# Edge loop of a graph network: products of two tiles in one VectorE instruction each

## What is computed

```
tpw = mlp(edge_feats)                      # per edge, 4 x 128
w1, w2, w3, w4 = jnp.split(tpw, 4, axis=-1)
s0, s1 = x0[sender], x1[sender]            # 128 and 128 x 3
y0, y1 = edge_attrs[:, 0:1], edge_attrs[:, 1:4]
p1 = w1 * s0 * y0
p2 = (w2 * s0)[:, :, None] * y1[:, None, :]
p3 = w3[:, :, None] * s1 * y0[:, None, :]
p4 = w4 * jnp.einsum('eum,em->eu', s1, y1) / SQRT3
msg0 = jax.ops.segment_sum(concat(p1, p4), receiver)
msg1 = jax.ops.segment_sum(concat(p2, p3), receiver)
```

## Time and profile before

| | |
|---|---|
| median of three runs | 1691.36 us (1691.3 to 1697.8) |
| the profiled execution, span from first to last instruction | 1690.4 us |
| PE busy | 1478.5 us, 87% |
| DVE busy | 1306.6 us, 77% |
| ACT busy | 739.0 us, 44% |
| POOL busy | 498.2 us, 29% |
| mean granted TensorE clock | 0.946 |
| first and last L2072 of the edge loop | 698.9 and 1055.4 us |

### The profile page before, as it was taken

How to read it: one execution, slowest core, us unless ns; L and a number is a source line. 1 busy time by engine, 2 the same in 40 slices (tenths; PEclk the granted TensorE clock), 3 DMA queues, 4 the chain that set the end, 5 groups by cost and what they waited for, 6 DMA issues and landing times.

```text
span 1690.4 us, 24268 instructions
## 1 busy us (share of the span) xinstructions
PE 1478.5 (87%) x7869; PEld 805.5 (48%) x7869; DVE 1306.6 (77%) x2051; ACT 739.0 (44%) x1580; POOL 498.2 (29%) x496
## 2 busy tenths in 40 slices
PE   2888998367888787899999999979999999999997
PEld 1465445213333335566555565855544444444443
DVE  8786999997999997499898999697577656632232
ACT  1285666267555555355454555441244333402000
POOL 1788888710011012356555664000000000002000
PEclk9988999678999997799999999979999999999999
DMA  4101000143121102466565667000111201220000
GB/s 143 42 6 9 6 7 7 36 146 114 43 68 40 65 16 82 129 184 183 165 183 165 182 184 148 1 1 26 50 50 50 70 30 58 66 74 1 13 19 30
DMA packets 66890, 122.06 MB, mean 72 GB/s; under 512 B 12753, under 2 KB 31299, under 8 KB 66702
## 3 DMA queue, kind: packets, MB, share of 16 engines
q0 software_dynamic: 23408, 59.71, 14.1%
q1 hardware_dynamic: 41976, 57.57, 10.5%
q10 hardware_dynamic: 1446, 4.03, 0.7%
HBM read 105.85 MB, written 15.23 MB: 72 GB/s over the span
## 4 chain that ended last, share of the span: by engine, by line
PE 53%; DVE 16%; POOL 14%; issue 10%; ACT 4%; DMA 2%; DVEq 1%; ACTq 0%; POOLq 0%
PE PS L1240 18%; POOL recs L656 14%; PE PS L1116 8%; DVE arena L1923 6%; PE PS L1205 5%; PE PS L1306 5%; PE PS L1102 5%; DVE arena L1919 3%; ACT arena L1578 3%; PE PS L1291 2%; PE PS L1302 2%; PE PS L1167 1%; DVE cnt_d L1704 1%; DVE arena L2123 1%; PE PS L976 1%
## 5 line engine op out<-in xcount | busy, mean ns | idle before, releaser
L1240 PE MATMUL PS<-arena 128*125 128x512 f32 x640 | 275.0, 592 | 0.0
L656 POOL DMA_INDIRECT recs<-arena x170 | 244.3, 1437 | 89.9 <-issue 89.0
L1578 ACT ACTIVATE arena<-arena,gslot 128x32 f32<-128x32 f32 x832 | 185.1, 308 | 172.5 <-PE PS L1116 89.6
L1116 PE MATMUL PS<-arena 128*32 128x128 f32 (+1 forms) x3328 | 235.0, 311 | 16.2 <-issue 8.0
L721 POOL DMA_INDIRECT arena<-xup,gidx x208 | 197.5, 949 | 147.6 <-issue 69.9
L1116 PEld LDWEIGHTS PS<-arena 128*32 128x32 f32 x3328 | 176.9, 111 | 127.1 <-issue 68.6
L1028 PE MATMUL PS<-arena 125*128 125x512 f32 (+1 forms) x480 | 190.5, 534 | 44.1 <-DVE arena L1923 43.9
L2072 DVE TENSOR_TENSOR arena<-PS,arena 128x768 f32<-128x768 f32 x208 | 196.7, 946 | 0.0
L1240 PEld LDWEIGHTS PS<-arena 128*125 128x125 f32 x640 | 120.1, 188 | 154.6 <-issue 154.1
L1028 PEld LDWEIGHTS PS<-arena 125*128 125x128 f32 x480 | 86.0, 191 | 148.4 <-issue 78.0
L728 POOL CAST arena<-cnt_s 125x1250 f32<-125x1250 uint16 x10 | 12.5, 1302 | 473.1 <-PE PS L1240 473.1
(11 more groups left out here) (341 smaller groups left out, 2149.9 us busy)
## 6 DMA issues: line engine op xcount, KB each, us to landing
arena<-in_spline_wT SPq DMA_DIRECT2D x16, 1024.0 KB, 5.4
arena<-uv_rows SPq DMA_DIRECT2D x14, 610.4 KB
arena<-h_rows SPq DMA_DIRECT2D x26, 256.0 KB
h_rows<-arena SPq DMA_DIRECT2D x24, 256.0 KB, 2.8
arena<-xup,gidx POOLq DMA_INDIRECT x208
recs<-arena POOLq DMA_INDIRECT x170
xup<-arena SPq DMA_DIRECT2D x10, 250.0 KB
out<-x_sb SPq DMA_DIRECT2D x10, 250.0 KB
```

What stands on the lines that cost most here:

```text
L656: pool.indirect_dma_start(out=recs, out_offset=bass.IndirectOffsetOnAxis(pos[:, c:c + 1], 0), in_=rec[:, c, :], in_offset=None).then_inc(s ...
L1116: ins = t.matmul(PS[quad * DB:(quad + 1) * DB, bank, o0 * MUL:o0 * MUL + w], sel4[:, s, v * DB:(v + 1) * DB], prod[:, s, c0 * MUL:c1 * MUL ...
L1240: return t.matmul(PS[:NP, y2_bank(half, b), :], lhs[:, (k * HB + b) * NP:(k * HB + b + 1) * NP], w[:, k * D:(k + 1) * D], start=(first and ...
L1578: ins = A(sel4[:, s, y * DB:(y + 1) * DB], eq4[:, m // 4, s * DB:(s + 1) * DB], ACT.Copy, scale=gslot[:, par, c + R_Y + y:c + R_Y + y + 1])
```

## The change

`products(m)`, which made the products of one tile with two instructions of 256 and 768 elements, becomes `pair_products(k)`, which makes those of a pair with two instructions of 512 and 1536 elements. Their PSUM banks (0, 1 or 6, 7), their slots in `ring` and their halves of `prod` lie side by side, so one access pattern with one more dimension covers both tiles. It waits for both tiles' gathers and for both path weights, and counts `s_prod_ok` up by two at its end. The comparison stays on DVE, ahead of each second pair. `two_groups` now issues the products of pair k + 1, then the sums of both tiles of pair k. Nothing is changed in `add_sums`, nor in the loops of PE, ACT, POOL and SP. Besides, the counters s_xt1, s_xt2, s_xt3 and s_cols2 go away: those waits count on from s_xt and s_cols with an offset (x1_transposes, linear_up, x2_transposes, x3_transposes, evac_T, x2_in, x3_in, and L1617, L2128); and three helper functions that nothing called are deleted.

```
-            def products(m, par, n, n_pair, n_gath):
-
-                s = m % 4
-                if m == 0:
+            def pair_products(k, par, n, n_pair, n_gath):
+
+                m, s = 2 * k, 2 * k % 4
+                if k == 0:
                     dve.wait_ge(s_gidx_ok, n_pair)
-                if m % 4 == 0:
+                if k % 2 == 0:
                     dve.wait_ge(s_sel_ok, n + (2 * TP - 4))
...
-                xg = ring[:, m, :].rearrange("p (q n) -> p q n", q=4)
-                w = PS[:, (0, 1, 6, 7)[s], :].rearrange("p (q n) -> p q n", q=4)
-                pr = prod[:, s, :].rearrange("p (h q n) -> p h q n", h=2, q=4)
+                xg = ring[:, m:m + 2, :].rearrange("p t (q n) -> p t q n", q=4)
+                b0 = (0, 6)[k % 2]
+                w = PS[:, b0:b0 + 2, :].rearrange("p t (h g n) -> p t h g n", h=2, g=2)
+                pr = prod[:, s:s + 2, :].rearrange("p t (h q n) -> p t h q n", h=2, q=4)
                 dve.wait_ge(s_gath[m], n_gath)
-                dve.wait_ge(s_tpw_ps, n + (2 - m % 2))
-                v.tensor_tensor(pr[:, :, 0, :], w[:, 0:3:2, :], xg[:, 0:1, :].to_broadcast([128, 2, MUL]), ALU.mult)
-                v.tensor_tensor(pr[:, :, 1:4, :], w[:, 1:4:2, :].unsqueeze(2).to_broadcast([128, 2, 3, MUL]),
-                                xg[:, 1:4, :].unsqueeze(1).to_broadcast([128, 2, 3, MUL]), ALU.mult).then_inc(s_prod_ok, 1)
+                dve.wait_ge(s_gath[m + 1], n_gath)
+                dve.wait_ge(s_tpw_ps, n + 2)
+                v.tensor_tensor(pr[:, :, :, 0, :], w[:, :, :, 0, :], xg[:, :, 0:1, :].to_broadcast([128, 2, 2, MUL]), ALU.mult)
+                v.tensor_tensor(pr[:, :, :, 1:4, :], w[:, :, :, 1, :].unsqueeze(3).to_broadcast([128, 2, 2, 3, MUL]),
+                                xg[:, :, 1:4, :].unsqueeze(2).to_broadcast([128, 2, 2, 3, MUL]), ALU.mult).then_inc(s_prod_ok, 2)
...
             def two_groups(i, par, last=False):
-                for m in range(TP):
-                    if m + AHEAD < TP:
-                        products(m + AHEAD, par, i * (2 * TP) + (TP * par + m + AHEAD), None, i * 32 + 16 * (par + 1))
+                for k in range(GT):
+                    if k + 1 < GT:
+                        pair_products(k + 1, par, i * (2 * TP) + (TP * par + 2 * k + 2), None, i * 32 + 16 * (par + 1))
                     elif not last:
...
-                    if m % 4 == 0:
-                        word = dve.value_load(gpk[0:1, m // 4, bass.ds(i * 2 + par, 1)], min_val=0, max_val=64 ** 4 - 1)
-                    add_sums(m, i * (2 * TP) + (TP * par + m), word)
...
+                    if k % 2 == 0:
+                        word = dve.value_load(gpk[0:1, k // 2, bass.ds(i * 2 + par, 1)], min_val=0, max_val=64 ** 4 - 1)
+                    for m in (2 * k, 2 * k + 1):
+                        add_sums(m, i * (2 * TP) + (TP * par + m), word)
```

More of the change, by code:

```diff
@@ L733, in _ @@
             t = nc.tensor
[L735 to L755, removed]
             def uv_transposes(src, nr, done, b0):
@@ L1048, in x1_transposes @@
                 if b >= 2:
-                    pe.wait_ge(s_xt1_cp, b - 1)
+                    pe.wait_ge(s_xt_cp, NB + b - 1)
                 for k in range(4):
@@ L1053, in x1_transposes @@
                     ins = t.transpose(PS[:, 4 + b % 2, k * 128:k * 128 + NP], src, ident[:NP, :NP])
-                ins.then_inc(s_xt1_ps, 1)
+                ins.then_inc(s_xt_ps, 1)
             def linear_up(b):
-                pe.wait_ge(s_xt1_cp, b + 1)
+                pe.wait_ge(s_xt_cp, NB + b + 1)
                 if b == 0:
@@ L1142, in x2_transposes @@
                 if b >= 2:
-                    pe.wait_ge(s_xt2_cp, b - 1)
+                    pe.wait_ge(s_xt_cp, 2 * NB + b - 1)
                 for k in range(KT):
                     ins = t.transpose(PS[:, 6 + b % 2, k * 128:k * 128 + NP], x_sb[:, b, k * 128:(k + 1) * 128], ident[:NP, :NP])
-                ins.then_inc(s_xt2_ps, 1)
+                ins.then_inc(s_xt_ps, 1)
             def msg_transposes(b):
@@ L1174, in _ @@
                 x2_transposes(b)
-            pe.wait_ge(s_xt2_cp, NB - 1)
+            pe.wait_ge(s_xt_cp, 3 * NB - 1)
             quad_rows(wa2, xT2, 0, 0, s_r4_ps)
             quad_rows(wa2, xT2, 1, 1, s_r4_ps)
-            pe.wait_ge(s_xt2_cp, NB)
+            pe.wait_ge(s_xt_cp, 3 * NB)
             quad_rows(wa2, xT2, 2, 2, s_r4_ps)
@@ L1186, in _ @@
                 ins = t.matmul(PS[:NP, 6, b * 2:(b + 1) * 2], rows4b[:, b * NP:(b + 1) * NP], sel_r[:, 0:2], start=True, stop=True)
-            ins.then_inc(s_cols2_ps, 1)
+            ins.then_inc(s_cols_ps, 1)
             def half_rows(hf):
@@ L1274, in x3_transposes @@
                 if b >= 2:
-                    pe.wait_ge(s_xt3_cp, b - 1)
+                    pe.wait_ge(s_xt_cp, 3 * NB + b - 1)
                 for k in range(KT):
                     ins = t.transpose(PS[:, 1 + b % 2, k * 128:k * 128 + NP], x_sb[:, b, k * 128:(k + 1) * 128], ident[:NP, :NP])
-                ins.then_inc(s_xt3_ps, 1)
+                ins.then_inc(s_xt_ps, 1)
             x3_transposes(0)
@@ L1282, in _ @@
             for c in range(NB):
-                pe.wait_ge(s_xt3_cp, c + 1)
+                pe.wait_ge(s_xt_cp, 3 * NB + c + 1)
                 if c == 0:
@@ L1320, in ln_sqrt, with evac_T @@
                 A(rstd[:, b:b + 1], mv[:, b, 1:2], ACT.Sqrt, bias=epsc[:NP, :]).then_inc(s_ln_sd, 1)
-            def evac_T(dst, done, copied, banks, layer=0, then=None):
+            def evac_T(dst, done, copied, banks, n0, layer, then):
                 if layer:
@@ L1329, in evac_T @@
                         ln_sqrt(layer, b + 1)
-                    act.wait_ge(done, b + 1)
+                    act.wait_ge(done, n0 + b + 1)
                     A(dst[:, :, b * NP:(b + 1) * NP],
@@ L1562, in xup_out @@
                     A(w2T[:, b - 4, :], PS[:, b % 2, :], ACT.Copy).then_inc(s_wa_cp, 1)
-            evac_T(xT1, s_xt1_ps, s_xt1_cp, (4, 5), 1, xup_out)
+            evac_T(xT1, s_xt_ps, s_xt_cp, (4, 5), NB, 1, xup_out)
             act.wait_ge(s_wt_ps, 2 * KT + 3)
@@ L1587, in x2_in @@
             def x2_in(b):
-                act.wait_ge(s_xt2_ps, b + 1)
+                act.wait_ge(s_xt_ps, 2 * NB + b + 1)
                 A(xT2[:, :, b * NP:(b + 1) * NP],
-                  PS[:, 6 + b % 2, :].rearrange("p (k n) -> p k n", k=KT)[:, :, 0:NP], ACT.Copy).then_inc(s_xt2_cp, 1)
+                  PS[:, 6 + b % 2, :].rearrange("p (k n) -> p k n", k=KT)[:, :, 0:NP], ACT.Copy).then_inc(s_xt_cp, 1)
             m5 = msgT.rearrange("p (h j) (b n) -> p h j b n", h=2, n=DB)
@@ L1616, in _ @@
                 A(st_b[:, n0:n1], PS[:NP, 3 + q, 0:n1 - n0], ACT.Copy).then_inc(s_st_ok, 1)
-            act.wait_ge(s_cols2_ps, 1)
-            A(sc[:, :, 0:2], PS[:NP, 6, 0:NB * 2].rearrange("p (b n) -> p b n", n=2), ACT.Copy).then_inc(s_cols2_cp, 1)
+            act.wait_ge(s_cols_ps, 2)
+            A(sc[:, :, 0:2], PS[:NP, 6, 0:NB * 2].rearrange("p (b n) -> p b n", n=2), ACT.Copy).then_inc(s_cols_cp, 1)
             HW = HB * NP
@@ L1669, in x3_in @@
             def x3_in(b):
-                act.wait_ge(s_xt3_ps, b + 1)
+                act.wait_ge(s_xt_ps, 3 * NB + b + 1)
                 A(xT3[:, :, b * NP:(b + 1) * NP],
-                  PS[:, 1 + b % 2, :].rearrange("p (k n) -> p k n", k=KT)[:, :, 0:NP], ACT.Copy).then_inc(s_xt3_cp, 1)
+                  PS[:, 1 + b % 2, :].rearrange("p (k n) -> p k n", k=KT)[:, :, 0:NP], ACT.Copy).then_inc(s_xt_cp, 1)
             for b in range(HB):
@@ L2127, in half_terms @@
                 if hf == 0:
-                    dve.wait_ge(s_cols2_cp, 1)
+                    dve.wait_ge(s_cols_cp, 2)
                 link(v.tensor_tensor(mt2[:, bs], mx1[:, bs], sc[:, bs, 0], ALU.add))
```

17 lines of the change are left out of this document (3 added, 14 removed).

## The result

The changed kernel takes **1713.2 us** (median of four runs, 1707.9 to 1715.9) against 1692.6 (four runs, 1691.3 to 1697.8). The ratio is 1.0122, with a 95% interval of 1.0089 to 1.0154: slower by 15 to 26 us. The forecast was 1720, range 1705 to 1735.

The account below looks back on a forecast made before the run. PE and DVE, both nearly full, ran the edge loop at 3.28 us a pair through waits between them; DVE becomes the bound. 1691.4 plus 19.7 + 1.7 + 1 + 7 = +29 gives 1720 us, range 1705 to 1735.

Parts of the forecast that it names:

- The bare wait: On DVE in the edge loop, a pair's second sum starts 0.79 us behind the first, not 0.33: 0.46 us a pair.
- The merged products: On DVE, merged products take 0.60 and 1.67 us, together 2.27 instead of 2.40, saving 0.13 a pair; fourth dimension 0.
- DVE's pair: DVE in the edge loop: 3.39 us a pair, 3.59 with the comparison, average 3.49 against 3.28: +19.7 and +1.7 us.
- The start: At the loop's start the first merged pair needs both gathers, its first product complete at 702.4 instead of 699.8: +1 us.
- Later signals: In the edge loop, PE's signal for a pair's first sum 0.3 us too late, plus DVE register work: +7 us.
- Rival B: In the edge loop, PE's signals are held in each pair and register work adds 0.1: 1738 us, chance 20%.
- The stretches at half clock: Edge loop stretches at 1.2 GHz: 4.9 us a pair, over 3.49, so the change adds nothing there.
- rival C: Edge loop: loss half hidden, with no half clock, late signals free and sums 0.70 apart: 1697 us, chance 6%.
- Rival A: Edge loop: the back-to-back wait between sums costs nothing, sums 0.33 apart, PE's 3.05 decides: 1670 us, chance 4%.

Follow-up runs that it names:

- e_order: The kernel before with the new order alone (products of two tiles, then both sums), every product still of one tile: 1718.9 us, ratio 1.0164.
- e_wait: The changed kernel with the wait for the sum before hung on the sum itself, address registers computed ahead of it: 1703.1 us, ratio 1.0076.
- e_after_nogath: The changed kernel without the gathers of its edge loop: 1700.7 us beside 1661.2, ratio 1.0230.
- e_nogath: The kernel before without the gathers of the edge loop: 1660.0 us beside 1690.9, ratio 0.9812.
- e_before_wait: The kernel before, gathers kept, with the wait for the sum before hung on the sum itself, on chip 4: 1662.1 us beside 1658.6, ratio 1.0003.
- e_split_nogath: The changed kernel with a sum between the two merged products, without the edge loop's gathers: 1661.3 us beside 1661.2, ratio 0.9995.
- e_wait_nogath: The changed kernel with the wait for the sum before hung on the sum itself, without the edge loop's gathers: 1663.2 us beside 1661.2, ratio 1.0016.

## Why the prediction was right

- *The bare wait.* The step of two sums was taken from the loop's end, 0.79, and is 0.78 in 87 of the 104 pairs. e_order shows it without the merge, e_wait takes 0.32 of it away and leaves 0.46. So of the 0.45 that it costs over 0.33, 0.32 is the address computed behind the wait, and 0.13 is left with the wait hung on the sum itself.
- *The merged products.* 0.60 and 1.67 were taken from a line through two points; the starts give 0.61 and 1.66. Their lengths are 0.68 and 1.75. The fourth dimension costs nothing that shows.
- *DVE's pair.* 3.39 and 3.59 forecast, 3.38 and 3.58 measured. Over 3.28 that is 0.20 for 103 steps, +20.6 us (forecast 19.7 + 1.7).
- *The start.* From the first gather's issue to the end of the first pair's products it was 6.2 us (695.07 to 700.36 + 0.95) and is 7.3 (698.79 to 704.35 + 1.75): +1.1, forecast +1.
- *Later signals* was 7 us and had its mechanism wrong. Late signals cost the changed kernel's steady pairs nothing, since e_after_nogath has the very same ones. They were not held less (89%). The prediction took the signal at 3.6 us behind the products for the one that DVE wants at 3.31. In the changed kernel's trace the signal at 3.6 (median 3.63) is the second scatter's, which DVE wants at 4.07 or later; the first scatter's comes at 1.36 (median; 95 of 100 by 2.8) and is wanted at 3.3. What came in its place are the turns, which look like time of DVE's sequencer (part of it is idle put down to "issue"): 0.46 at ten of the 12 turns of the loop's body, 0.77 at the first and 0.12 at the last, +5.5 us, the same without gathers. That 7 us were forecast and 5.5 came, from another cause, is luck. Rival B is out.
- *The stretches at half clock* were to stay as they were. The two at 824 and 896 went: below full clock there is only the loop's start, mean 0.73 from 690 to 722. What the loop has over its steady pairs and turns (3.28 before; 3.48 and the turns now) fell from 355.1 - 103 x 3.28 = 17.3 to 374.0 - 103 x 3.48 - 5.5 = 10.1 us, a gain of 7. It lies mainly in stalls: two of them, at 821 and 894, with the half clock behind them, made the pairs of the kernel before 10.5 us longer, and the changed kernel has one, of 3.5 us. That is the part of rival C that came true; its other parts did not. But C had PE full ahead of these stretches, and the trace says otherwise. PE's matmuls stand apart before the clock falls: PE is busy 72% of 818 to 822 and 59% of 822 to 826, and the granted clock falls within that second stretch (mean 0.72); it is busy 57% of 894 to 898, where the mean clock is 0.68. So the half clock came with the stalls. Both are gone where no signal is late (e_nogath, e_before_wait). Why the changed kernel, whose signals are late, has one stall and not two, no run shows.

Sum: 20.6 + 1.1 + 5.5 - 7.2 = +20.0 us; from the first gather's issue to the last sum the loop went from 364.0 to 384.1 us. The last term is what was left over, so the sum had to close. Outside the loop the first gather came 3.7 us later and what follows the last sum took 2.1 us less. The other kernels' traces of the same condition have their first gather anywhere from 692.7 to 699.2, so this is scatter and not the change. So the forecast of +29 was right in its mechanism, the bare wait, and 8 us too high, nearly all of it the gain of 7 that it didn't see.

There is a second way to read the 21 us, which only the runs made plain. The kernel before had 31 us of slack in its loop from PE's late signals (356.6 against 325.4 us without gathers). The changed kernel's own DVE work is 38 us longer (103 x (3.48 - 3.16) + 5.5; its loop without gathers is 365.3 - 325.4 = 40 us longer), and about half of that fell into the slack. In the chip's other condition there is no such slack: the changed kernel without gathers stands at 1700.7 beside 1661.2, and the whole kernel should lose about as much, some 2%. It wasn't run there.

Rival A rested on the Trainium skill ("VectorE: DVE Perf Modes", The DRAIN you can't avoid), by which a semaphore behind each of several Vector instructions is free. The page doesn't say whether its copies waited for each other, and for instructions that do, the runs don't agree: two sums of which the second waits for the first are 0.46 apart with no register work between them, and a sum and the product that follows it without such a wait are 0.33 apart. That is 0.13 us at each, far less than the 0.45 that it came to with the register work, but not nothing.

None of the kernels that do the whole work beats the one before. e_split_nogath and e_wait_nogath only draw level, although their DVE work is merged: what merging saves (0.13 a pair) goes into the turns and what is left of bare waits.

## What to carry to other kernels

Before merging two instructions, look what stood between them: here 0.13 us a pair was saved, and a wait that had been covered by the products between two sums came out, at 0.45 us. Where a chain on one engine must wait for its own last result, compute the address ahead of the wait and hang the wait on the instruction that needs it. And measure a kernel that joins PE and indirect DMAs more than once: the same program was 1690.9 us and later 1661.2 us on chip 3.

## What the runs showed of the hardware

- PE's semaphore signals can be held while POOL runs indirect DMAs. In the traces of one condition 64 to 97% of those beside a gather of the edge loop came over 0.1 us late, the slowest twentieth of all signals in the kernel before by 2.5 us or more; with no indirect DMA of POOL beside them (156 signals between 140 and 420 us) none was late. In four later traces none was late: three on chip 3, whose traces have indirect DMAs only ahead of the edge loop, up to 346 us, and e_before_wait on chip 4, with the loop's gathers too. In the first condition this and what came with it cost the kernel before 31 us.
- The kernel before had two stalls in the middle of its loop, in which DVE stood idle for 3.7 and 4.7 us and after whose start the granted clock fell to half, 1.2 GHz, for some 6 us. They are in neither e_nogath nor e_before_wait: they went with the late signals. The mean clock from 690 to 1060 us is 0.95 in the kernel before and 0.99 in e_before_wait.
- A sum that waits for the sum just before it starts 0.46 us behind it, for 0.33 without such a wait, if the wait hangs on the instruction, and 0.78 if three register instructions stand behind the wait.
